# Mask of the first attention block: a row of the stacked score operands in place of a bias of the exponential

## The reference, cut to what matters

```python
def _L0_xattn_ref(hidden_states, audio_tokens, attention_mask, Wq, bq, Wk, bk, Wv, bv, Wo, bo, ...):
    q, k, v = ...                                     # 4 x 16 heads x 256 or 512 x 16
    scores = einsum('bhsd,bhtd->bhst', q, k) / sqrt(16)
    # positions with attention_mask != 0 are left out; probabilities are made with exp, clipped at exp(-50) and exp(50)
    ctx = einsum('bhst,bhtd->bhsd', probs, v)
    delta = residual_scale * (ctx @ Wo.T + bo)        # then a layer norm
```

## Time and profile before

| | |
|---|---|
| median of 3 runs | 1154.88 us |
| the three runs | 1154.19, 1154.88, 1156.72 us |
| span of the profiled execution | 1153.3 us |
| PE, DVE, ACT, POOL busy, share of the span | 88, 70, 49, 37% |
| the 128 exponentials of this block (line 1058) | 80.0 us in all, 695 ns in the mean |
| the 256 exponentials of the others (line 1060) | 144.1 us in all, 597 ns in the mean |

### The profile page before, as it was taken

How to read it: one execution, slowest core, us unless ns; L and a number is a source line. 1 busy time by engine, 2 the same in 40 slices (tenths; PEclk the granted TensorE clock), 3 DMA queues, 4 the chain that set the end, 5 groups by cost and what they waited for, 6 DMA issues and landing times.

```text
span 1153.3 us, 19199 instructions
## 1 busy us (share of the span) xinstructions
PE 1015.4 (88%) x6456; PEld 764.3 (66%) x6456; DVE 807.4 (70%) x1639; ACT 570.5 (49%) x1129; POOL 431.4 (37%) x519
## 2 busy tenths in 40 slices
PE   4899868989877998789999875899999989998998
PEld 3566547877766877565664664566555568887887
DVE  6477758678866668688886765877675266776766
ACT  3788754444433442236667442265655534444443
POOL 5524414355303455523220324323210134554553
PEclk8999989899998999879999988899999889999999
DMA  6936624454320478754520336736511134455554
GB/s 180 249 93 155 124 72 128 143 162 132 121 92 1 128 135 204 167 93 121 126 53 21 118 75 142 149 88 94 122 34 31 49 109 126 155 151 152 159 156 122
DMA packets 82059, 136.43 MB, mean 118 GB/s; under 512 B 11565, under 2 KB 40518, under 8 KB 79546
## 3 DMA queue, kind: packets, MB, share of 16 engines
q1 hardware_dynamic: 71034, 101.93, 29.9%
q0 software_dynamic: 10944, 33.45, 17.1%
HBM read 113.41 MB, written 22.97 MB: 118 GB/s over the span
## 4 chain that ended last, share of the span: by engine, by line
PE 59%; DVE 17%; DMA 6%; issue 6%; ACT 6%; POOL 4%; SPq 1%; DVEq 0%; ACTq 0%; POOLq 0%
PE psum L616 36%; PE psum L909 7%; PE psum L876 6%; PE psum L885 5%; DMA ff_raw<-in_ff 4%; ACT probs L1058 2%; DMA weights_out<-combine 1%; DVE nmx L1371 1%; DVE nmx L1374 1%; DVE ff_s L1997 1%; DVE nmx L1372 1%; PE psum L835 1%; POOL ff_wl L1958 1%; DVE probs L1465 1%; PE psum L717 1%
## 5 line engine op out<-in xcount | busy, mean ns | idle before, releaser
L616 PE MATMUL psum<-ff_xh,ff_wh 128*128 128x512 f32 x424 | 176.8, 417 | 22.3 <-POOL ff_wl L1958 17.6
L2014 DVE TENSOR_TENSOR ff_hl<-ff_h,ff_hh 128x512 fp32r<-128x512 f32 x114 | 121.9, 1069 | 94.5 <-ACT ff_hh L1899 94.1
L1958 POOL TENSOR_TENSOR ff_wl<-ff_raw,ff_wh 128x512 fp32r<-128x512 f32 x92 | 120.6, 1311 | 171.7 <-ACT ff_wh L1910 171.4
L1060 ACT ACTIVATE probs<-psum 128x512 f32<-128x512 f32 x256 | 144.1, 597 | 78.8 <-PE psum L876 75.1
L876 PE MATMUL psum<-queries,keys 128*128 128x512 f32 x384 | 155.7, 436 | 12.9 <-ACT probs L1058 6.1
L616 PE MATMUL psum<-ff_xh,ff_wl 128*128 128x512 f32 x392 | 156.7, 400 | 0.0
L1910 ACT ACTIVATE ff_wh<-ff_raw 128x512 fp32r<-128x512 f32 x92 | 58.0, 630 | 181.9 <-DMA ff_raw<-in_ff 179.1
L616 PE MATMUL psum<-ff_wh,ff_hh 128*128 128x256 f32 x456 | 131.1, 291 | 9.3 <-DVE ff_hl L2014 9.2
L885 PE MATMUL psum<-keys,queries 128*128 128x512 f32 x256 | 118.2, 478 | 18.6 <-DVE nmx L1372 8.3
L616 PE MATMUL psum<-ff_wh,ff_hl 128*128 128x256 f32 x456 | 129.9, 289 | 0.0
L1963 POOL TENSOR_TENSOR ff_wl<-ff_raw,ff_wh 128x256 fp32r<-128x256 f32 x92 | 91.3, 992 | 61.7 <-ACT ff_wh L1917 60.6
(11 more groups left out here) (263 smaller groups left out, 2199.5 us busy)
## 6 DMA issues: line engine op xcount, KB each, us to landing
ff_w<-weights_out SPq DMA_DIRECT2D x94, 256.0 KB
ff_raw<-in_ff SPq DMA_DIRECT2D x92, 256.0 KB, 3.6
ff_raw<-in_ff SPq DMA_DIRECT2D x106, 128.0 KB, 2.1
keys_out<-keys_turned SPq DMA_DIRECT2D x24, 512.0 KB, 3.7
keys<-keys_out POOLq DMA_DIRECT2D x48, 256.0 KB, 5.1
queries_out<-queries_turned SPq DMA_DIRECT2D x24, 256.0 KB, 4.3
keys<-keys_out POOLq DMA_DIRECT2D x48, 128.0 KB, 5.4
queries<-queries_out POOLq DMA_DIRECT2D x32, 192.0 KB, 4.0
```

Of the source, the lines that this page charges most:

```text
L616: last = eng.matmul(dst, lhs[i](k), rhs[j](k), start=start and n == 0, stop=stop and n == groups * len(pairs) - 1, skip_group_check=True)
L1060: ins = eng.activation(dst, src, ACT.Exp, scale=SCALE)
L1958: then(eng.tensor_tensor(ff_wl[:, slot, 0:2 * D], raw(n, slot)[:, 0:2 * D], ff_wh[:, slot, 0:2 * D].bitcast(F32), ALU.subtract), "f_w1r")
L2014: then(eng.tensor_tensor(ff_hl[:, slot, :], ff_h[:, slot, :], ff_hh[:, slot, :].bitcast(F32), ALU.subtract), "f_hr")
```

## The change

The mask becomes row `AUG + 15` of each head's 64 rows: the keys' stack holds the mask there (0 or -2^100 for each position), the queries' stack holds ones, so the score matmul adds it. The exponential takes no bias. The mask is loaded first of all by SP, as 16 rows of 128 positions; DVE turns it as its first work; SP writes it to memory (`masked`), before the load of the values' weights; and `keys_in` of this block reads it into the stack with 2 more transfers per half (16 in the block). The ones are 2 transfers per buffer by POOL. One of POOL's small loads in `start` goes.

```diff
@@ tiles
+    mask_rows = nm_st[32:32 + B * KT, :].bitcast(F32)
+    mask_i = o_tmp[32:32 + B * KT, 0:P].bitcast(I32)
-    aug0 = sb("aug0", [P, B * KT])
-    mask_i = sb("mask_i", [P, B * KT], I32)
+    masked = nc.dram_tensor("masked", (B, M), F32, kind="Internal").ap()
@@ exponentials
-                    eng.wait_ge(sems["aug_done"], 1)
...
-                if blk == 0:
-                    ins = eng.activation(dst, src, ACT.Exp, scale=SCALE, bias=aug0[:, KT * c + kt:KT * c + kt + 1])
-                else:
-                    ins = eng.activation(dst, src, ACT.Exp, scale=SCALE)
-                then(ins, "p_exp")
+                then(eng.activation(dst, src, ACT.Exp, scale=SCALE), "p_exp")
@@ POOL: constant_rows, keys_in
-                    r, n = 64 * m + AUG, HD - 1 if two else HD
+                    r, n = 64 * m + AUG, HD if blk == 2 else HD - 1
...
+            def ones_row(b):
+                src = a["aug_q"][HD - 1:HD].rearrange("r (j c) -> r j c", j=NP)
+                for m in range(2):
+                    r = 64 * m + AUG + HD - 1
+                    move(qst[buf(b)][r:r + 1, m, :, :], src, f"d_au{buf(b)}")
...
+                if blk == 0:
+                    if b == 0:
+                        eng.wait_ge(sems["d_masked"], 16)
+                    src = masked[b:b + 1, :].rearrange("r (one c) -> r one c", one=1).to_broadcast([1, JJ, M])
+                    for m in range(2):
+                        r = 64 * m + AUG + HD - 1
+                        move(kst[buf(b)][r:r + 1, pairs, :], src, f"d_r{buf(b)}{ph}")
@@ steps of POOL
+                elif st[0] == "au" and blk == 0:
+                    if st[1]:
+                        eng.wait_ge(sems["s_zeroed"], 1)
+                        constant_rows(st[1])
+                    ones_row(st[1])
@@ SP
+        load(mask_i, a["mask_keys"], "d_mask0")
         load(w_raw[:, WK], a["w0"][:, WK], "d_w01")
...
         context_and_tokens(1)
+        eng.wait_ge(sems["mask_done"], 1)
+        load(masked.rearrange("b (k p) -> (b k) p", p=P), mask_rows, "d_masked")
         load(w_raw[:, WV], a["w0"][:, WV], "d_w02")
@@ DVE
+        eng.wait_ge(sems["d_mask0"], 16)
+        link(eng, "dve", eng.tensor_scalar(mask_rows, mask_i, 0.5, 1.0, ALU.is_gt, ALU.subtract))
+        then(eng.tensor_scalar(mask_rows, mask_rows, -FAR, None, ALU.mult), "mask_done")
         then(eng.memset(qst[0][:, :].bitcast(F32), 0.0), "s_zeroed")
@@ masks
-            link(eng, "dve", eng.tensor_scalar(aug0[:, :], mask_i[:, :], 0.5, 1.0, ALU.is_gt, ALU.subtract))
-            link(eng, "dve", eng.tensor_scalar(aug0[:, :], aug0[:, :], -FAR, None, ALU.mult))
```

More of the change, by code:

```diff
@@ L585, in flamingo @@
              ("d_small d_ident d_bias d_w2 d_w2n d_rows0 d_rows2 d_rows3 d_rows3a d_gate d_mask1 d_down d_fu0 d_fu1 d_fd0 d_fd1 d_fw0 d_fw1 d_wm "
-              "d_cn0 d_cn1 d_out d_kw d_qw d_nw d_r00 d_r01 d_r10 d_r11 d_nr0 d_nr1 d_kept d_aq d_au0 d_au1").split())
+              "d_cn0 d_cn1 d_out d_kw d_qw d_nw d_r00 d_r01 d_r10 d_r11 d_nr0 d_nr1 d_kept d_mask0 d_masked d_aq d_au0 d_au1").split())
     START = ("v_init ct_l0 ones_done beta_used bp_used z_done g_tanh ct_h ct_l w0_h w0_l bias_h bias_l w2_l "
-             "w3_l aug_done q_zeroed s_zeroed").split()
+             "w3_l aug_done mask_done q_zeroed s_zeroed").split()
     CHAINS = ["dve", "pool"]
@@ L631, in landed @@
     def landed(blk, b):
-        return 16 * 8 * (B // 2 * (0, 2, 3).index(blk) + b // 2 + 1)
+        masks = B // 2 if blk else b // 2 + 1
+        return 16 * (8 * (B // 2 * (0, 2, 3).index(blk) + b // 2 + 1) + 2 * masks)
     def constants(blk, which):
-        return 16 * ({0: 2, 2: 4, 3: 8}[blk] - 2 * which)
+        return 16 * ({0: 4, 2: 6, 3: 10}[blk] - 2 * which)
     def attention(blk):
@@ L1052, in exponentials @@
                     w(eng, "o_full", n // 4 - 2)
-                part, k = divmod(u, 4)
-                kt = 2 * (part % 2) + k % 2
+                k = u % 4
                 dst = probs[:, n // 4 % 3, k % 2, 2 * (k // 2):2 * (k // 2) + 2, :].rearrange("p h c -> p (h c)")
                 src = psum[:, score_banks[n % len(score_banks)], :]
-                if blk == 0:
-                    ins = eng.activation(dst, src, ACT.Exp, scale=SCALE, bias=aug0[:, KT * c + kt:KT * c + kt + 1])
-                else:
-                    ins = eng.activation(dst, src, ACT.Exp, scale=SCALE)
-                then(ins, "p_exp")
+                then(eng.activation(dst, src, ACT.Exp, scale=SCALE), "p_exp")
             def evacuate(c, g):
@@ L1175, in do @@
                     pass
-                elif st[0] == "au" and (blk or st[1]):
+                elif st[0] == "au" and blk == 0:
[3 more added lines that the diff above has]
+                    ones_row(st[1])
+                elif st[0] == "au":
                     if two and st[1] == 0:
@@ L2560, in start @@
             then(eng.memset(bias_raw[:, :, :], 0.0), "z_done")
-            for dst, src in ((mask_i[:, :], a["mask_keys"]), (lens_i[:, :], a["lens"].to_broadcast([P, 1])),
+            for dst, src in ((lens_i[:, :], a["lens"].to_broadcast([P, 1])),
                              (g_all[:, :], a["gates"].to_broadcast([P, 8])),
@@ L2625, in others @@
             context(3)
-            eng.wait_ge(sems["d_small"], 16 * 5)
+            eng.wait_ge(sems["d_small"], 16 * 4)
             then(eng.activation(g_all[:, :], g_all[:, :], ACT.Tanh), "g_tanh")
@@ L2802 @@
     arrays["text_at"] = np.where(key < IMG, -2.0 ** 30, key - IMG).astype(np.float32).T
-    arrays["mask_keys"] = v["mask_BxS2_ik0"].reshape(B * KT, P).T
+    arrays["mask_keys"] = v["mask_BxS2_ik0"].reshape(B * KT, P)
     arrays["mask_row"] = v["mask_BxS2_bk0"].reshape(1, B, M)
```

## The result

The changed kernel takes **1164.78 us** in the median of 6 runs (1159.68 to 1168.06), the kernel before 1153.05 (1151.26 to 1156.72) beside it. The ratio is 1.0093, 95% interval 1.0068 to 1.0118: slower by 8 to 14 us. The prediction was 1155.4 with a range to 1159.4. The measured time is 9.4 us above the forecast and 5.4 above the range, so the prediction is **wrong**.

The account below looks back on a forecast made before the run. No single engine was taken to bound the first attention block; its chain is shared by PE, ACT, DVE and POOL. Terms 1.9 + 0.3 + 1.1 - 0.4 - 2.4 = +0.5 us on 1154.88 gave 1155.4 us, range 1152.4 to 1159.4.

Parts of the forecast that it names:

- Cost: the wait at DVE's start: DVE's first memset waits for the mask's load and two operations, starting near 3.5 us instead of 1.67: +1.9 us.
- Gain: two DVE operations in masks: Two mask operations leave DVE's path ahead of the statistics before batch 0's keys: -0.4 us.
- Cost: the mask rows of batch 0: Mask rows issued behind batch 0's keys may land after them: 0 to +1.1 us, taken as +0.3.
- Gain: the exponentials: First attention block: 128 exponentials each 0.09 us shorter without bias, about 31 on the chain: -2.4 us, ceiling 2.8.
- Cost: POOL's queue at batch 3: Four more POOL issues delay the root before ff_xn, partly offset by a cheaper root: +1.1 us, between 0.5 and 2.3.
- a colder PE: Rival: batch 0's longer wait puts PE at its slower level for early work there: +3.0 us, 1157.9; chance 0.05.
- Batches 1 and 2: Idle time at batch 2 covers the added issues, and batch 1 is fed early: nothing, up to +1 us.
- POOL's queue decides: Rival: slow POOL issues, stretched by DVE's clips, cost at batches 0, 2, 3, plus a late start: +6.2, 1161.1; chance 0.27.
- The two other rivals: ACT was the limit, start's delay hidden: -3.2 us, 1151.7, chance 0.10; exponential no shorter without bias: +2.9, 1157.8, 0.03.
- The first score at 44 or later: Sign of a wrong forecast, meaning late mask rows; the forecast had the first score near 42.6 us.
- the block's end moved by over 2 us: Sign of a wrong forecast, either way; the forecast had the first attention block's end within 1 us of before.

Follow-up runs that it names:

- e4: Changed kernel with POOL's two large memsets held until DVE's two mask operations are done: 1163.44 us, ratio 1.0074.
- e9: e6b with DVE's mask operations behind batch 0's ctx_lo and w_lo, and the mask's load at the end of SP's start loads: 1156.83 us, ratio 1.0015.
- e2: Changed kernel with DVE's two mask operations moved from the head to behind the first layer norm's statistic: 1159.50 us, ratio 1.0031.
- e1: Kernel before with only the bias left out of the 128 exponentials, so no mask is applied: 1153.65 us, ratio 0.9973.
- e8b: Kernel before, bias and old mask kept, plus four transfers of zeros at batch 3, two behind each half's keys: 1157.60 us, ratio 1.0022.
- e5b: e2 without the 16 transfers of mask rows, zeros loaded instead, so no mask is applied: 1153.51 us, ratio 0.9992.
- e6b: e2 with mask rows moved whole, 8 transfers in all, well before each batch's keys: 1155.89 us, ratio 1.0005.
- e3: Changed kernel with the mask rows issued in front of the keys of each half: 1165.82 us, ratio 1.0074.
- e7b: e2 with POOL doing the root of ff_xn between the two halves of batch 3's keys: 1153.05 us, ratio 0.9978.

## Why the prediction was wrong, point by point

**"Cost: the wait at DVE's start", +1.9, is the step that failed.** The term was a wait for a load plus 0.6 us of operations, and e4 shows this to be right where POOL is quiet: +2.03. In the changed kernel DVE's memset starts 7.2 us later, 5.2 more than that, since the operations fall on POOL's two memsets. Of the 7.2, 1.7 come back at once: the cast of ident_r takes 0.23 us now, as it no longer runs beside them. By the means of two profiles POOL's first issue of batch 0's keys starts 5.9 us later (31.09 and 31.61, now 37.46 and 37.09), where the prediction had +1.5 with the two operations of masks taken off. This miss of 4.4 us is about half of the whole. It was to be seen in the trace of before: the same cast ended at 7.94, with POOL's memset (7.86):

```profile
6.05 1.89 DVE L2659 CAST ident_r<-ident_raw 128x128 fp32r<-128x128 f32 x1
```

In e4, where POOL's memsets are later, the cast takes 1.92 us again and ends at 10.00, with the second memset (9.92). The prediction used the rule on the shared ports in the Trainium skill (SBUF — State Buffer, SBUF: two separate sides) for POOL's transfers alone. The page says the same of any operation of GpSimd against such an operation of DVE, an exclusive lock for the whole instruction; with 0.22 us in e4 against 2.01 and 3.53 in after the traces agree. Its other half, that whichever starts first has the ports, agrees with after, where POOL's memsets start at 0.79 and 4.35 and the operations at 2.36 and 4.41; e9's rows (13.82, 14.04 and 14.35) can't decide it. I priced the two operations from rows taken at 28 us, when POOL was idle.

A smaller step went wrong with it: the prediction had SP's wait for `mask_done` over before SP reached it. In after SP is done with the issue ahead of it at 6.13 and issues the store at 7.97, and the load of the values' weights behind it at 8.34 instead of 5.71. No cost of that is seen: in e2 this load is issued later still, at 9.41, with the first score at 41.14.

**"Gain: two DVE operations in masks", -0.4: right.** In the chain of waits of before 0.45 us lie between the last operation on the bias and the next one of the statistics (27.16 to 27.61), and 0.03 in after (33.94 to 33.97).

**"Cost: the mask rows of batch 0", +0.3: not contradicted.** A mask row is last to land in after (9.39 us, with PE waiting). But from POOL's first issue of batch 0's keys to the first score it is 9.8, 12.5, 9.3, 8.5, 11.9, 10.8 and 9.8 us in the seven profiles without mask rows at this place (before twice, e1, e8b, e5b, e6b, e9), 10.4 in the mean, and 12.0, 10.3, 10.2, 10.5, 11.2 and 10.8 in the six with them (after twice, e2, e3, e4, e7b), 10.8 in the mean. A difference of 0.4 is far inside the scatter. One profile of each would have said 2.2.

**"Gain: the exponentials", -2.4: right in kind, its size seen in part.** 90 ns each, as predicted. A to R is 73.9 to 74.3 us in the three profiles with the bias and 72.1 to 73.4 in the ten without: -1.4 for three of the four batches. The granted clock of that stretch doesn't explain it: where it is 0.98, A to R is 74.0 and 74.3 with the bias and 72.4 to 72.8 without. X to F holds the rest, and goes with the clock (below): at 0.96 it is 42.8 in before and 42.4 in e7b.

**"Cost: POOL's queue at batch 3", +1.1: 2.2.** The direction and the cheaper root were right (1.05 for 1.94). The issues were mis-sized: twelve took 3.1 us more than eight, 0.77 each and not 0.57, so that 3.1 - 0.9 = 2.2 is left, just under the upper bound of 2.3 that was given. The prediction's own 1.4 had been taken down to 1.1 without a number for it. In before one clip of DVE fell on the issues. In after there are two (125.28, 128.34), one in each half, and the halves' keys take 2.65 and 3.04 us for four issues where two issues take 1.0. That was the rival's argument. That clips make the issues longer is argued from these rows; no run moved a clip. That the queue costs the 2.2 from R to X is shown by e8b (four issues alone, 8.7 to 10.9) and e7b (the place of the root alone, back to 8.7).

**Then PE waits, and its granted clock falls.** The stretch from 125 to 140 us: start and end, length, busy time (and instructions) of PE, PEld, DVE, ACT and POOL, then the granted clock, the DMA share and GB/s. In before, and in after:

```profile
125.00:140.00 15.00, 12.48 (x112) 7.76 (x113) 10.27 (x22) 11.31 (x21) 1.20 (x2) 1.00 0.51 102
```

```profile
125.00:140.00 15.00, 11.03 (x88) 4.83 (x80) 8.25 (x19) 9.27 (x20) 10.56 (x15) 0.89 1.13 168
```

0.89 stands in this stretch in all five profiles with an R to X of 10.9 (after twice, e2, e4, e8b), where PE waits 2.6 to 3.6 us, and 1.00 in all eight others: for a part of the stretch PE is granted 1.2 GHz instead of 2.4. But the wait alone doesn't decide it. In e3 PE waits 2.57 us (to 134.93) and has 1.00 there, and from 140 to 150 us the clock is 0.83 in before's second profile and in e1 (and 0.84 and 0.78 from 150 to 165), with no wait of PE over 1.4 us between 125 and 150.

X to F goes with the clock over its whole length, whatever the kernel: 42.4 to 42.8 us at 0.95 to 0.97 (five profiles), 43.0 and 43.6 at 0.93, 43.6 at 0.92, 44.1, 44.1 and 44.3 at 0.89, 45.1 at 0.87 and 46.2 at 0.84. That also places e1, which has its low clock later in the stage. So the mean of -0.1 for X to F compares two profiles of before at 0.96 and 0.87 with two of after at 0.92 and 0.89, and it says nothing of the change. Against before's first profile after is 0.8 and 1.3 us longer, against its second 1.5 and 1.0 shorter. How much of a low clock in this stage is due to the change stays open. The prediction's rival *a colder PE* looked for this at batch 0, where it isn't to be told from before (0.87 and 0.92 up to the first score in before, 0.90 and 0.89 in after).

**"Batches 1 and 2", nothing: right.** At batch 2 the twelve issues took 8.4 us (93.89 to 102.26) for 5.60, the 2.8 us that were priced, and the idle time in front of the root swallowed them: A to R fell all the same.

**What was not predicted: F to end.** The change has nothing to do there, and the text let the block's end pass through whole. By the means it is +2.4 us. The eight profiles with mask rows moved by transfers have 982.3 to 990.5, 988.5 in the mean; the five without, 983.4 to 987.1, 985.3 in the mean. The difference isn't in one place of the later blocks, and e7b with the lowest value of all has the rows. The granted clock over this stage is 0.95 and 0.96 in the two profiles of before and 0.95 and 0.94 in those of after, which is a hint and no more. Whether it is an effect or chance stays open; 2.4 of the 9.1 us are not explained.

**The forecast as a sum.** Predicted +0.5: start 1.5, rows 0.3, exponentials -2.4, batch 3 1.1. Measured by two profiles each, +9.1: start 5.9, rows 0.0, exponentials -1.4 (A to R), batch 3 2.2, X to F -0.1, F to end 2.4. The rival *POOL's queue decides* (1161.1) came nearest, in part by luck: its start cost of 2.9 was that of a late load, where 5.9 were lost to another cause; its costs at batch 2 and of the rows were not seen; and at batch 3 it gave nothing back for the root, which came 0.9 cheaper. The range was too narrow for another reason as well: its upper bound for the start was taken from how late a load may land, and nothing bounded the operations behind it. The two other rivals did not come: nothing became faster, and the exponential without bias is shorter.

**The signs that were named.** "The first score at 44 or later" and "the block's end moved by over 2 us" both came: 49.4, and 176.4 for 166.2 (175.1 for 171.8 in the second profiles).

**No version beats the kernel before measurably.** The loss can be taken away (e6b, e7b, e9), with ratios of 0.9978 to 1.0015 whose intervals all hold 1. e7b is the lowest, and its interval still reaches 1.0004. The gain of the exponentials, even without any mask at all, stands at 0.9973 (0.9942 to 1.0003).

## What to carry to other kernels

Price an operation from a row that runs beside the same neighbours as it will: the two mask operations cost 0.22 us at one place and 2.0 and 3.5 at another, and a small operation whose end falls together with the end of another engine's instruction is a hint to look for. Work added to a queue in front of something that others wait for can cost most of its length (2.2 of 3.1 us at batch 3, but nothing at batch 2, where idle time stood behind it), so move the thing that is waited for ahead of it (e7b) or the added work away (e6b), before asking whether the transfers are dear. Before a wait for a transfer is counted as a cost, profile the unchanged kernel twice: the first score of before moved by 3.2 us by itself. And before the lengths of a stage of PE are compared, put its granted clock beside them.

## What the runs showed of the hardware that was not expected

- Operations of DVE on 16 x 128 elements (0.22 us each alone) are held by a memset on POOL until it ends: 2.01 and 3.53 us, 2.04 and 3.53 in the second profile, 2.91 in e9 (where an issue of POOL runs ahead of the memset). A cast of DVE to fp32r on 128 x 128 is held in the same way: 1.89 us beside the memset in before, 1.92 in e4, 0.23 in after. A memset of DVE beside POOL's is not (3.47 us both beside it and behind it, in e4 and after).
- A memset of DVE behind such an operation begins 0.92 us after the operation's end, in after as in e4, with nothing in the trace that it waits for.
- The granted clock of one stage differs between two executions of the same program, and the stage's length with it: from X to F before takes 42.8 us in one profile (0.96) and 45.1 in the other (0.87).
- The landing of the last transfer in front of the first score takes 8.15 and 10.85 us in the two profiles of before, 9.39 and 7.75 in those of after: for the same work, up to 2.7 us more or less.
